# Audio tower layer on one core: how the last two tiles leave the pipeline

## The reference, cut to what matters

```python
for _ in range(2):
    shared_ctrl = gelu(ctx @ shared_w1 + b) @ shared_w2 + b      # one branch for all rows
    ctrl = experts(ctx_e, flat_idx, ...)                         # the two chosen experts of each row
    # for each of the three branches, ctrl = (a, b, g):
    v_next = sigmoid(a) * v - softplus(b) * (x - mu)
    x_next = x + 0.1 * sigmoid(g) * v_next
    # weighted over branches, then halt = sigmoid(gelu(x @ halt_w1) @ halt_w2)
    integrated = integrated + halt * (x_next - integrated)
refined = gelu(integrated @ refine_w1 + b) @ refine_w2 + b
out = xf + integration_weight * refined
```

## Time and profile before

| | us |
|---|---|
| median of 3 runs (765.49 to 766.56) | 765.87 |
| the profiled execution's own time | 766.59 |
| its span, first to last instruction | 764.8 |
| TensorE busy | 724.5 (95%) |
| VectorE busy | 626.5 (82%) |
| ScalarE busy | 598.1 (78%) |
| GpSimd busy | 377.8 (49%) |
| mean granted TensorE clock | 0.976 |

### The profile page before, as it was taken

One profiled execution on the slowest core, in us unless ns is written; L12 is line 12 of the kernel. 1 busy time (PEld: TensorE's weight loads), 2 busy tenths in 40 slices (PEclk: granted clock), 3 DMA queues, 4 the chain that ended last, 5 costly groups with the idle time before them and its releaser, 6 DMA issues.

```text
span 764.8 us, 14327 instructions
## 1 busy us (share of the span) xinstructions
PE 724.5 (95%) x4516; PEld 615.4 (80%) x4516; DVE 626.5 (82%) x1430; ACT 598.1 (78%) x1382; POOL 377.8 (49%) x438
## 2 busy tenths in 40 slices
PE   5667999999999999999999999999999999999976
PEld 3446788888888888888888888887988888887876
DVE  3857788988988988988988988988889889888762
ACT  4765778788788788888888878888888888776672
POOL 1426456555555555555645545555555564563210
PEclk9888999999999999999999999999999999999995
DMA  8300000000000000000000000000000000000000
GB/s 330 124 15 1 8 1 17 6 22 8 15 22 1 21 21 3 20 23 1 22 22 1 22 21 1 21 22 1 21 21 1 8 8 2 8 9 1 8 8 14
DMA packets 11611, 17.27 MB, mean 23 GB/s; under 512 B 1232, under 2 KB 10504, under 8 KB 11024
## 3 DMA queue, kind: packets, MB, share of 16 engines
q1 hardware_dynamic: 11536, 16.35, 6.3%
HBM read 13.20 MB, written 3.15 MB: 21 GB/s over the span
## 4 chain that ended last, share of the span: by engine, by line
PE 89%; DVE 4%; ACT 3%; issue 2%; POOL 1%; DMA 1%; SPq 0%; ACTq 0%; POOLq 0%; DVEq 0%
PE ctl L495 23%; PE ctl L511 11%; PE ctl L472 5%; PE ctl L501 4%; PE ctl L514 4%; PE cd L593 4%; PE pa L593 4%; PE cd L472 3%; PE cd L666 3%; PE ctl L562 3%; PE ctl L481 2%; PE pa L588 2%; PE cd L588 2%; PE pb L593 2%; PE ctl L482 2%
## 5 line engine op out<-in xcount | busy, mean ns | idle before, releaser
L375 POOL TENSOR_TENSOR hm_lo<-gl,mexp 128x256 fp32r<-128x256 f32 x144 | 128.1, 914 | 100.0 <-DVE gl L1257 96.5
L495 PE MATMUL ctl<-w2e_hi,hm_hi 128*128 128x512 f32 (+1 forms) x432 | 158.6, 376 | 0.1
L495 PE MATMUL ctl<-w2e_lo,hm_hi 128*128 128x512 f32 (+1 forms) x432 | 150.8, 362 | 0.0
L495 PEld LDWEIGHTS ctl<-w2e_hi,hm_hi 128*128 128x128 f32 x432 | 82.2, 190 | 22.2 <-DVE hm_hi L1243 7.9
L511 PE MATMUL ctl<-w2e_hi,hm_lo 128*128 128x512 f32 (+1 forms) x432 | 99.9, 357 | 0.0
L1243 DVE TENSOR_TENSOR hm_hi<-ge,mexp 128x256 fp32r<-128x256 f32 x144 | 89.2, 634 | 12.4 <-ACT ge L946 9.4
L965 ACT ACTIVATE work<-ctl 128x256 f32<-128x256 f32 (+1 forms) x144 | 69.6, 484 | 35.4 <-PE ctl L514 27.4
L495 PEld LDWEIGHTS ctl<-w2e_lo,hm_hi 128*128 128x128 f32 x432 | 82.4, 191 | 10.6
L511 PEld LDWEIGHTS ctl<-w2e_hi,hm_lo 128*128 128x128 f32 x432 | 74.6, 188 | 13.7 <-POOL hm_lo L375 0.3
L381 POOL TENSOR_TENSOR rg_lo<-rg,rg_hi 128x512 fp32r<-128x512 f32 x23 | 33.2, 1445 | 74.9 <-ACT rg_hi L902 74.8
L917 ACT ACT_TABLE_LOAD x49 | 62.9, 1283 | 0.9
(11 more groups left out here) (210 smaller groups left out, 2061.4 us busy)
## 6 DMA issues: line engine op xcount, KB each, us to landing
work<-params_dram SPq DMA_DIRECT2D x3, 1152.0 KB, 12.6
xT<-turned_dram SPq DMA_DIRECT2D x24, 128.0 KB, 2.2
out_dram<-y SPq DMA_DIRECT2D x24, 128.0 KB, 1.7
xa<-x_dram SPq DMA_DIRECT2D x16, 128.0 KB, 2.3
par<-params_dram SPq DMA_DIRECT2D x1, 1280.0 KB, 10.3
work<-params_dram SPq DMA_DIRECT2D x2, 512.0 KB, 10.9
xa<-x_dram SPq DMA_DIRECT2D x8, 119.0 KB
par<-params_dram SPq DMA_DIRECT2D x1, 512.0 KB, 15.7
```

What stands on the lines that cost most here:

```text
L375: TT(hm[1][:, j, c, :], gl[:, c, part, :], pairs(tile, j, c), ALU.mult).then_inc(done, 1)
L495: mm(dst[:, a:z], hm[0][:, j, c, :], w2e[i][:, c, a:z], start=(c == 0 and i == 0), stop=False)
```

## The change

It concerns tiles 21 to 23 alone.

- ACT: in the `last_in` slot branch 0 of tile 23 gets its softplus right behind tile 22's, under the same table. `last_units` replaces the last two `unit` calls of tile 23: tanh of branch 1, softplus table, softplus of branches 1 and 2 straight from PSUM, the Gelu/tanh table, tanh of branch 2. ACT copies no x2 of tiles 22 and 23 any more.
- DVE: tile 23's gates are formed branch by branch (`last_gates`, `last_product`), and DVE copies x2 of tiles 22 and 23 out of PSUM (`second_state`). It also forms `rg_lo` of tile 22 (`late_refine_lo`), which POOL did.
- PE: in slot 25 tile 22's low products (`refine_lo`) come after tile 23's transposes and first refine layer. That layer goes in two halves into two PSUM tensors (`pd` and `pb`), and the second layer of tile 23 (`refine_last`) is: high and low products of the first half, then of the second. Its Gelu and parts live in `ge` and `gh`, which are free by then, and its sum in `pc`.

The diff, cut to its core:

```diff
 def refine_in(o):
+    if o.newest():
+        passed(pe, th2_sb, o)
+        hidden(pd, P, r1, range(0, 2), x2T, KD, rl1_ps)
+        hidden(pb, P, r1[:, :, 2:REF // P, :], range(0, 2), x2T, KD, rl1_ps)
+    else:
+        hidden(refine_ps(o), P, r1, range(REF // P), x2T, KD, rl1_ps)
+def refine_last(o):
+    for i, half in enumerate((range(0, 2), range(2, REF // P))):
+        passed(pe, rgh_sb, o, step=1 + i)
+        for w in range(2):
+            for c in half:
+                mm(refined(o), last_rgp[0][:, c, :], r2[w][:, c, :], ...)
+        passed(pe, rgl_g, o, step=1 + i)
+        for c in half:
+            last = mm(refined(o), last_rgp[1][:, c, :], r2[0][:, c, :], ...)
+    last.then_inc(rl2_ps, 1)
...
 # PE slot
-if o.exists() and not last_in:
+if o.newest():
+    refine_last(o)
+elif o.exists() and not last_in:
     refine_hi(o)
+    if m.newest():
+        passed(pe, x2T_sb, m, back=1)
+        second_turned(m)
+        refine_in(m)
     refine_lo(o)
...
+def last_units(n):
+    passed(act, u2_ps, n, per=BR, step=2)
+    AF(tan[n.s][:, 1:BR, 1, :], ctl[0][:, D:3 * D]..., ACT.Tanh, scale=0.5)
+    nc.scalar.preload_act_table_set("softplus")
+    AF(rb[n.s][:, 1, :], ctl[0][:, 0:D], ACT.Softplus).then_inc(u2_sb, 1)
+    passed(act, u2_ps, n, per=BR)
+    AF(rb[n.s][:, 2, :], ctl[1][:, 0:D], ACT.Softplus).then_inc(sp2_sb, 1)
+    table_of_gelus()
+    AF(tan[n.s][:, 1:BR, 2, :], ctl[1][:, D:3 * D]..., ACT.Tanh, scale=0.5).then_inc(u2_sb, 1)
...
 # ACT slot
-if o.exists():
-    if m.exists() and not n.exists():
-        softplus_of(m, t)
-        passed(act, rl1_ps, o, back=1)
-        state(x2T, pc, D, o, x2T_ps, x2T_sb)
-        table_of_gelus()
+if o.newest():
+    last_refine_units(o)
+elif o.exists():
     refine_units(o)
...
 if not t.exists():
     softplus_of(m, t)
+    passed(act, u2_sb, n, per=BR, step=1)
+    AF(rb[n.s][:, 0, :], rb[n.s][:, 0, :], ACT.Softplus)
     table_of_gelus()
...
 # DVE slot
+if m.newest():
+    last_gates(m, 1)
+    second_state(o)
+    for j in range(2):
+        last_product(m, j)
+    link(V.tensor_tensor(both, tan[m.s][:, 0:2, 0, :], tan[m.s][:, 0:2, 1, :], ALU.add))
+    last_gates(m, 2)
+    passed(dve, sp2_sb, m)
+    last_product(m, 2)
+    V.tensor_tensor(both, both, tan[m.s][:, 0:2, 2, :], ALU.add).then_inc(sums_v, 1)
...
+if last_in:
+    gates(m)
+    velocity_gates(m)
+    last_gates(n, 0)
...
+if m.newest():
+    second_state(m)
+    late_refine_lo(o)
+if last_in:
+    output(o)
 if o.newest():
-    last_refine_lo(o)
-if o.exists() and not t.exists():
+    last_refine_lo(o, 0)
+    output(o.at(-1))
+    last_refine_lo(o, 1)
     output(o)
```

More of the change, by code:

```diff
@@ L252, in refined @@
         def refined(o):
+            if o.newest():
+                return pc[:, D:2 * D]
             return ctl[0][:, 3 * D:4 * D] if o.low < LATE else pa[:, 0:D]
+        last_rg, last_rgp = ge[:, :, 0, :], [gh[:, :, part, :] for part in range(2)]
+        last_gw = pq[:, :, 0, :]
         par_in = [sem(f"par_in{i}") for i in range(len(_KEPT))]
@@ L391, in slot @@
                 e, f, n, m, o = t.at(2), t.at(1), t.at(-1), t.at(-2), t.at(-3)
+                last_in = n.exists() and not t.exists()
                 if f.exists():
@@ L432, in slot @@
                     TT(vu[t.s][:, 1, :], x1[t.s][:, :], pv("mu"), ALU.subtract).then_inc(u1_g, 1)
-                if o.exists() and not t.exists() and not o.newest():
+                if o.exists() and last_in:
                     refine_lo(o)
@@ L555, in refine_hi @@
                     passed(pe, e_sb, Tile(BATCH - 1, NS - 1).at(2), per=2)
[L556 to L562, removed]
+                for w in range(2):
+                    for c in range(REF // P):
+                        mm(refined(o), rgp[0][:, c, :], r2[w][:, c, :], start=(w == 0 and c == 0), stop=False)
             def refine_lo(o):
@@ L892, in refine_units, with last_refine_units @@
                     last = AF(rg[:, c, :], refine_ps(o)[:, c * P:(c + 1) * P], ACT.Gelu, bias=par[:, a:a + 1])
[L893 to L898, removed]
-                    last.then_inc(rg_sb, 1)
-                    passed(act, rg_sb, o)
-                    passed(act, rl2_ps, o, back=1)
-                    AF(rgp[0][:, :, :], rg[:, :, :], ACT.Copy).then_inc(rgh_sb, 1)
+                last.then_inc(rg_sb, 1)
+                passed(act, rg_sb, o)
+                passed(act, rl2_ps, o, back=1)
+                AF(rgp[0][:, :, :], rg[:, :, :], ACT.Copy).then_inc(rgh_sb, 1)
+            def last_refine_units(o):
+                passed(act, gl2_v, o)
+                passed(act, hm2_v, o, per=3)
+                for i, src in enumerate((pd, pb)):
+                    passed(act, rl1_ps, o, step=1 + i)
+                    for k in range(2):
+                        c = 2 * i + k
+                        a = OFF["rb1"][0] + c
+                        last = AF(last_rg[:, c, :], src[:, k * P:(k + 1) * P], ACT.Gelu, bias=par[:, a:a + 1])
+                    last.then_inc(rg_sb, 1)
+                    passed(act, rg_sb, o, step=1 + i)
+                    both_of = slice(2 * i, 2 * i + 2)
+                    AF(last_rgp[0][:, both_of, :], last_rg[:, both_of, :], ACT.Copy).then_inc(rgh_sb, 1)
+            def last_units(n):
+                passed(act, u2_ps, n, per=BR, step=2)
+                AF(tan[n.s][:, 1:BR, 1, :], ctl[0][:, D:3 * D].rearrange("p (a d) -> p a d", a=2), ACT.Tanh, scale=0.5)
+                nc.scalar.preload_act_table_set("softplus")
[3 more added lines that the diff above has]
+                table_of_gelus()
+                AF(tan[n.s][:, 1:BR, 2, :], ctl[1][:, D:3 * D].rearrange("p (a d) -> p a d", a=2), ACT.Tanh,
+                   scale=0.5).then_inc(u2_sb, 1)
             def softplus_of(m, t):
@@ L1419, in slot @@
                     output(o)
-                if m.exists() and not last_in and not t.newest():
+                if m.exists() and t.exists() and not t.newest():
                     products(m)
```

62 lines of the change are left out of this document (38 added, 24 removed).

## The result

| | before | after |
|---|---|---|
| median of the first comparison (us) | 766.12 (765.49 to 766.56, 4 runs) | 759.11 (758.25 to 760.36, 4 runs) |
| ratio, 95% interval | | 0.9912 [0.9899, 0.9924] |
| the same two kernels in a later comparison | 765.19 (763.47 to 766.41, 23 runs) | 759.43 (758.58 to 762.67, 6 runs) |
| ratio, 95% interval | | 0.9943 [0.9923, 0.9963] |
| the profiled execution, its span | 766.59, 764.8 | 759.72, 757.9 |

A forecast was written before the change was run, and what follows sets the result against it. PE bounds the kernel until 742 us, then a ring of waits through ACT and PE, partly at low clock. Clock 3.7, early copy 2.1, order and halves 2.9: 765.87 - 8.7 = 757.2, plus 0.3 gives 757.5; range 756.5 to 761.2.

The forecast's parts named there:

- case B: Rival: PE's granted clock falls all the same in the last stretch; 758.8 to 760.8, middle 760; chance 0.45.
- case A: The forecast itself: PE stays at full clock through the tail; 757.5, alone spanning 756.5 to 758.5; chance 0.48.
- The early copy: DVE copies tile 22's x2 ahead of ACT's softplus; PE's first refine layer starts at 743.08, 2.1 us earlier.
- The sum: Tile 23's output sum starts at 753.4 instead of 762.13, 8.7 us off the span; 757.2, plus 0.3 gives 757.5.
- ACT and DVE up to x2: Softplus 0.38, copy 0.42, last tanh hidden by 0.5; tile 23's x2 ready at 748.3, 0.8 earlier.
- Order and halves, 2.9: Tile 22's low products behind tile 23's first layer, and tile 23's refine in halves: together 2.9 of 8.7 us.
- the clock's share: Part of the 8.7 us gain credited to PE's clock staying up in the tail: 3.7.
- The handoffs, 0.3: Every handoff in the tail was taken at its best value, so 0.3 was added to 757.2.
- PE keeps 2.4 GHz to the end: Clock step of the forecast: no fall in the tail, as idle stretches are at most 2.0; chance 0.48.
- B's last line: Clock falls only around 749.3, PE then works without a gap, and it may rise before the end: 758.8.
- About even: Odds on PE's clock staying up in the tail, a little in favour: 0.48 against 0.45 for a fall.
- Rival C: DVE becomes the bound up to tile 23's x2, 6.4 us becoming 12.8 under disturbance: slower, 767.7; chance 0.03.

The follow-up runs named there:

- experiment 4: Kernel before with only tile 22's x2 copied by DVE ahead of tile 23's gates, ACT's function order otherwise kept: median 766.13, ratio 1.0008.
- before, filled: Kernel before with unread matmuls (12, 7 and 2) in PE's idle stretches at the end: median 763.98, ratio 0.9979; profiled execution 764.47.
- after, again: Changed kernel without any edit, profiled in another execution: 759.24; median of its runs 759.43.
- the filled one: Changed kernel with 7 unread matmuls on PE behind tile 22's first refine layer: median 759.10, ratio 0.9930; profiled execution 759.44.

## Why the prediction came out as it did

The time lay in the range, and the middle of case B (758.8 to 760.8) is nearer to it than the forecast, which was case A.

- **The early copy: right.** First layer of tile 22 1.48 after the transposes (forecast 743.08 - 741.61 = 1.47). It was called 2.1 on its own; experiment 4 shows that the copy without ACT's new order brings the second layer forward by only 1.1 at full clock, and the median by nothing. The sum had assumed the reordering without saying so.
- **ACT and DVE up to x2: right.** Softplus 0.38, gate 0.35, copy 0.42, x2 at 748.43 for 748.3; the last tanh hidden. The load of 1.28 has nothing behind it: the next function begins 0.01 later. The Trainium skill's drain of 1.38 (ScalarE: Activation LUTs, What ACT_TABLE_LOAD costs) doesn't show here either.
- **Order and halves, 2.9: too much at full clock.** From T0, "before, filled" against "after, again": second layer 22 is 2.06 earlier, transposes 23 2.60, y(23) 3.62. So the copy with ACT's order is 2.06, what follows up to the transposes 0.54, the halves and the rest 1.02 (halves alone 0.88). The 2.9 was worked out with all of it at 1.2 GHz, where products in front of something cost nearly double (1.22 against 0.64 for four). Why the transposes gain only 0.54 is in the PE row of 748.58: they now wait for x2, so taking products away from in front of them gives no more. With the clock's share, 4.73 in the first profile where the split had 3.7, the tail at full clock is 8.35 shorter than in that profile; the forecast had 8.4. The walk through the tail was right in total, while its split into parts was not.
- **The handoffs, 0.3: right.** At full clock y(23) is 12.17 behind T0; the sum had 753.4 - 741.61 + 0.3 = 12.1.
- **The clock: the step that failed.** "PE keeps 2.4 GHz to the end" held in the second execution and not in the profiled one, which did what B's last line said: fall about 749.3, rise before the end. It cost 13.52 - 12.17 = 1.35. In the second execution the clock stayed up and the time was 759.24 all the same, because T0 was 0.9 later; the filled one at full clock, 1.1 later, had 759.44. So the 1.6 by which the median missed has two sources, the clock in the tail and an opening that the sum took for fixed. Of the seven profiled executions of the changed kernel and its unfilled variants the clock fell in four, of the three of before in all, of the three filled ones in none. "About even" fits that, but it is drawn anew in each execution.
- **What was not seen at all:** that the opening varies, and that the first profile's tail was 3 us dearer than that of two others. With 17.4 as its usual length the full-clock gain would have been set at 5.2. The medians differ by 5.8 to 7.0; with 6 or fewer runs on one side that is as far as they can be read.
- **Rival C was weighed rightly, and for the reason given.** DVE is slowed when POOL works beside it: one operation tripled. The change keeps away from it by moving the low part; with the part left on POOL C's mechanism costs 0.9, on one operation, not 6.4 on the whole chain.

The page TensorE: Matmul & The Clock Gate of the Trainium skill, section HAM oscillation, lays a fall to idle stretches alone. Against it stands the pair after and after again: idle stretches of 1.10, 1.90, 0.20 and 0.52 in one, of 1.11, 1.89, 0.20 and 0.52 in the other, a fall in the first only. That none of the three filled executions had a fall, against 8 of the 11 others, speaks for the page; three executions don't prove it.

What stays open: what sets the moment at which the clock changes in an execution. No run here set that moment.

## What to carry to other kernels

Before a tail is priced from one profile, look whether the granted clock changed in it, and take a second profile: here one kernel's tail was 20.5, 17.3 and 17.6. Price each edit at both clock levels, and count steps from an event that all versions share. A transfer between engines that makes an operand early is worth only what its consumer can use: ask what stands in front of the consumer on its own engine.

## What the runs showed of the hardware

- A DVE operation of 256 columns with two inputs from SBUF took 1.32 instead of 0.42 when POOL had begun a 512-column operation (1.34) 0.30 earlier, in two kernels alike, and 1.42 behind one (1.29) begun 0.15 earlier in a third; it ended 0.28 behind POOL's each time.
- The same stream of PE work with the same idle stretches, to 0.02 us, was followed by a fall to 1.2 GHz in one execution and by none in another.
- In the opening the changes of the clock wander too; T0 ran from 741.31 to 744.31, while from 80 to 740 us PE was busy 655.0 to 655.1 of 660 each time.
